# One staggered stage for spectrum, frequency gate and gated inverse, in place of three stages with a barrier after each

## The chip, the cores and the metric

The kernel runs on one core of a Trainium2 chip. The metric is the device time of one execution in microseconds (us), smaller is better. TensorE is called PE here as in the profile (its weight loads PEld), VectorE DVE, ScalarE ACT, GpSimd POOL; SP issues the DMAs.

## The reference

Four layers follow each other on x of shape (4, 64, 128, 128), float32. The change touches only the head of the first:

```
spec    = rfft2(x, norm='ortho')                    # 128 x 65 frequencies for each of 256 channel images
hid     = gelu(einsum('bchw,oc->bohw', abs(spec), fg_w1))      # 64 -> 16 channels at each frequency
gate    = sigmoid(einsum('bchw,oc->bohw', hid, fg_w2))         # 16 -> 64 channels
x_gated = irfft2(spec * gate, s=(h, w), norm='ortho')
xf      = x + x_gated
```

Everything after it (two patch convolutions of xf, an attention, the other three layers) is the same code before and after.

## The kernel before

The program is a sequence of stages. Each is a `Stage` with its own buffers and semaphores; at its end POOL clears the semaphores and all engines meet at a barrier, so no stage overlaps the next. Within a stage each engine runs its own instruction stream in order, and semaphores are the only link between them. `turns(eng, n)` emits the body once and then as a hardware loop for the other n - 1 turns.

The images lie in units of four (`G4`), 64 units in all, two units (s = 0, 1) a turn, 32 turns. A transform is two products with constant matrices of cosines and sines. `spectrum` loads a unit of x, multiplies it on the row axis by `c_h` (256 columns: 128 cosines and 128 sines), copies the result by ACT (L153), multiplies on the column axis by `c_w` (L141 and L142, 130 columns: 65 real and 65 imaginary), copies it by DVE (L169), squares it by ACT (L158), adds the squares by DVE (L173) and stores spectrum and power in DRAM. `frequency_gate` loads the power of all images with the channels of two images on the partitions, takes the root (L235), and runs the two channel products 416 frequencies at a time (L219, L228), Gelu and Sigmoid between them. `gated_inverse` loads spectrum, gate and x, multiplies (L315, two products of 128x260 a unit), transforms back over the rows with 256 output columns (L334, L335), ACT copies (L354), transforms over the columns with 65 rows of coefficients in two products (L342, L343), and DVE adds x (L322) while it reads PSUM.

All products are float32, and each appears in the trace as two matrix instructions, called passes below. One of 128x128 takes two passes, and so on.

## Time and profile before

| | |
|---|---|
| time, median of three runs | 8322.75 us (8309.79 to 8329.18) |
| the profiled execution: its time, its span | 8315.14 us, 8313.0 us |
| mean granted PE clock | 0.913 |
| `spectrum` | 0 to 280 us |
| `frequency_gate` | 280 to 422.5 us |
| `gated_inverse` | 422.5 to 870.5 us |
| all that follows | 870.5 to 8313 us |

The boundaries of the stages are the first DMA issue of the next one. The span is that of the trace. PEclk is the clock that the throttle granted to PE as a share of 2.4 GHz: 1.00 is 2.4 GHz and 0.50 is 1.2 GHz.

### The profile page before, as it was taken

Reading aid. Unit: us, or ns where it says so; the run is one execution under the profiler, and the core shown is the slowest. Engines: PE = TensorE matmul, PEld = TensorE weight load, DVE = VectorE, ACT = ScalarE, POOL = GpSimd, SP = SyncE. Lnnn points to the kernel's source line nnn. Section 1 sums busy time; section 2 is a strip of 40 time slices with the busy share of each in tenths; the row PEclk is TensorE's granted clock in tenths of the full one; section 3 lists DMA queues with packets and bytes.
Section 4 is the critical chain, followed back from the end, with each engine's and each line's share of the span. In section 5 each row is a group of like instructions: output and inputs, shape, how many; then the busy total and the mean of one; then the engine's idle time right before and its main releaser. Section 6 shows DMA issues by size and latency. Waiting matters only on the chain. (4 is left out here: it accounts for less than half of the span.)

```text
span 8313.0 us, 125384 instructions
## 1 busy us (share of the span) xinstructions
PE 7145.2 (86%) x38346; PEld 3824.7 (46%) x38346; DVE 5721.2 (69%) x5544; ACT 4038.9 (49%) x6602; POOL 3554.7 (43%) x2395
## 2 busy tenths in 40 slices
PE   8688584999999645987799999999989999999980
PEld 7356261333332542457422222222247777777760
DVE  2011014777776134831399999999979999999975
ACT  3411014666666124730266666666645555555532
POOL 0000000222222030000277777777768888888860
PEclk9788797999999877995699999999989999999995
DMA  9455526333333573343200000000000000000016
GB/s 154 125 140 137 106 50 221 94 102 98 100 100 92 128 241 111 102 133 91 47 14 14 14 14 13 14 14 14 9 14 11 10 9 9 9 10 9 10 28 190
DMA packets 724163, 582.48 MB, mean 70 GB/s; under 512 B 293562, under 2 KB 631105, under 8 KB 716505
## 3 DMA queue, kind: packets, MB, share of 16 engines
q1 hardware_dynamic: 723993, 580.38, 26.8%
q8 instruction: 87, 1.43, 0.1%
q14 instruction: 83, 0.68, 0.0%
HBM read 379.73 MB, written 197.83 MB: 69 GB/s over the span
## 5 line engine op out<-in xcount | busy, mean ns | idle before, releaser
L2646 POOL TENSOR_TENSOR spe_hc<-spe_hs,spe_cu 128x1024 f32<-128x1024 f32 x552 | 1289.6, 2358 | 293.8 <-DVE spe_hs L2843 293.8
L2242 POOL TENSOR_TENSOR spa_hc<-spa_hs,spa_cr 128x966 f32<-128x966 f32 x592 | 1224.7, 2069 | 426.7 <-DVE spa_hs L2516 410.6
L2516 DVE TENSOR_TENSOR_SCAN spa_hs<-spa_p_d,spa_hs,spa_bx 128x483 f32<-128x483 f32 x1168 | 1362.4, 1210 | 0.0
L2843 DVE TENSOR_TENSOR_SCAN spe_hs<-spe_p_d,spe_bx 128x1024 f32<-128x1024 f32 x552 | 1232.3, 2274 | 8.6 <-ACT spe_p_d L2792 7.9
L2720 PE MATMUL spe_p_y<-spe_idt,spe_hc 128*128 128x128 f32 x8832 | 1034.8, 276 | 0.0
L2720 PEld LDWEIGHTS spe_p_y<-spe_idt,spe_hc 128*128 128x128 f32 x8832 | 1012.0, 193 | 0.0
L1037 DVE TENSOR_REDUCE attention_nm<-attention_p_s 128x2 f32<-128x640 f32 x1024 | 789.0, 812 | 258.6 <-PE attention_p_s L894 257.5
L995 ACT ACTIVATE attention_pr<-attention_p_t 128x512 f32<-128x512 f32 x1280 | 710.6, 598 | 413.8 <-PE attention_p_t L917 285.7
L2427 ACT ACTIVATE spa_p_d<-spa_p_d,spa_av 128x483 f32<-128x483 f32 x1184 | 705.1, 634 | 409.5 <-PE spa_p_d L2299 407.5
L2792 ACT ACTIVATE spe_p_d<-spe_p_d 128x896 f32<-128x896 f32 x552 | 472.8, 900 | 845.8 <-PE spe_p_d L2705 845.4
L2299 PE MATMUL spa_p_d<-spa_du,spa_hot 32*128 32x483 f32 x2368 | 644.5, 619 | 58.0 <-DVE spa_hs L2516 48.8
L2502 DVE TENSOR_TENSOR spa_bx<-spa_br,spa_p_u 128x952 f32<-128x952 f32 x592 | 666.5, 1126 | 33.6 <-PE spa_p_u L2312 33.6
L2832 DVE TENSOR_TENSOR spe_bx<-spe_cu,spe_p_bc 128x2048 f32<-128x2048 f32 x276 | 631.5, 2288 | 51.8 <-ACT spe_cu L2784 17.0
L2312 PE MATMUL spa_p_u<-spa_du,spa_hot 32*128 32x483 f32 x2368 | 647.1, 621 | 0.7 <-DVE spa_bx L2502 0.5
L894 PE MATMUL attention_p_s<-attention_ks,attention_qs 96*128 96x320 bf16 x2048 | 454.5, 303 | 37.0 <-DMA attention_qs<-scratch_qp 20.9
L2299 PEld LDWEIGHTS spa_p_d<-spa_du,spa_hot 32*128 32x128 f32 x2368 | 182.1, 184 | 523.0 <-DVE spa_hs L2516 360.6
L1100 POOL TENSOR_TENSOR attention_on<-attention_os,attention_rc 128x512 f32<-128x512 f32 x128 | 162.6, 1270 | 589.4 <-DMA attention_rc<-scratch_den 379.4
L934 PE MATMUL attention_p_o<-attention_pr,attention_vs 128*32 128x512 f32 x3072 | 410.0, 606 | 0.4 <-ACT attention_os L1009 0.4
L917 PE MATMUL attention_p_t<-attention_qs,attention_ks 99*128 99x512 bf16 x1024 | 395.7, 387 | 4.7 <-DMA attention_qs<-attention_mr 3.0
L2705 PE MATMUL spe_p_d<-spe_wa,spe_dt 32*128 32x512 f32 x2208 | 376.0, 640 | 2.8 <-DVE spe_hs L2843 2.8
L415 POOL MEMSET conv_wb<- 128x4096 f32 x1 | 3.5, 3512 | 870.1 <-POOLq L38 870.1
L1869 PE MATMUL experts_p_x<-experts_fs,experts_wx 128*128 128x512 f32 x768 | 332.8, 596 | 47.4 <-DVE experts_bx L1895 47.4
(413 smaller groups left out, 11256.9 us busy)
## 6 DMA issues: line engine op xcount, KB each, us to landing
attention_qs<-scratch_qp SPq DMA_DIRECT2D x768, 64.0 KB, 2.6
attention_rc<-scratch_den SPq DMA_DIRECT2D x128, 256.0 KB
scratch_qp<-queries_parts SPq DMA_DIRECT2D x96, 256.0 KB, 2.3
spa_xt<-scratch_x SPq DMA_DIRECT2D x148, 121.5 KB, 2.6
scratch_spec<-spectrum_spc SPq DMA_DIRECT2D x64, 260.0 KB, 4.6
inverse_spec<-scratch_spec SPq DMA_DIRECT2D x64, 260.0 KB, 3.7
spectrum_xs<-in_x_dram SPq DMA_DIRECT2D x64, 256.0 KB, 5.1
inverse_xs<-in_x_dram SPq DMA_DIRECT2D x64, 256.0 KB, 3.3
```

Of the source, the lines that this page charges most:

```text
L995: nc.scalar.activation(pr[:, v, :], p_t[v % 2][:, :], ACT.Exp, scale=HD ** -0.5).then_inc(exp_done[v % 2], 1)
L1037: nc.vector.tensor_reduce(nm[:, c.u, t, 2 * s:2 * s + 2], p_s[s][:, :, 0:NK], AX.X, ALU.max, negate=True).then_inc(s_max[s], 1)
L2242: nc.gpsimd.tensor_tensor(hc[:, k % 8:k % 8 + 2, :], hs[:, k:k + 2, :], cr2[:, s % 2, :].unsqueeze(1).broadcast_to([128, 2, NA]), ALU.mult ...
L2299: mm = nc.tensor.matmul(p_d[(2 * j + e) % 4][:, 0:NA], hot[v, j // 2, :], du[v, s % 2, 0, :], start=True, stop=True)
L2312: mm = nc.tensor.matmul(p_u[:, e, 0:NA], hot[v, j // 2, :], du[v, s % 2, 1, :], start=True, stop=True)
L2427: nc.scalar.activation(p_d[k % 4][:, 0:NA], p_d[k % 4][:, 0:NA], ACT.Exp, scale=av2[:, k:k + 1]).then_inc(decay_ready, 1)
L2502: nc.vector.tensor_tensor(kept(bx[:, 2 * j:2 * j + 2, :]), b, kept(p_u[:, :, 0:NA]), ALU.mult).then_inc(bx_ready, 1)
L2516: nc.vector.tensor_tensor_scan(hs[:, k, v], p_d[k % 4][:, v], bx[:, k, v], 0.0 if start else hs[:, k, NA - 1:NA], ALU.mult, ALU.add).then_ ...
L2646: nc.gpsimd.tensor_tensor(hc[:, k, :, d, :].rearrange("p s d t -> p d s t"), hs[:, k % 2, d, :, :], rows, ALU.mult)\
L2720: mm = nc.tensor.matmul(p_y[:, px], hc[:, k, n].rearrange("p d t -> p (d t)"), idt[:, :], start=False, stop=(n == ST - 1))
L2832: nc.vector.tensor_tensor(bx[:, k % 2], steps, rows, ALU.mult).then_inc(bx_ready, 1)
L2843: nc.vector.tensor_tensor_scan(hs[:, k % 2, d].rearrange("p d s t -> p (d s t)"), p_d[h][:, :], bx[:, k % 2, d].rearrange("p d s t -> p (d ...
```

## The change

The three stages become one, `gated_frequencies`, a fully unrolled sequence of 97 steps with one unit u = t of the forward part and one unit v = t - 31 of the inverse part in step t. The gate of image b (16 units, u = 16b to 16b + 15) is spread over the half-steps k = 2t and 2t + 1 by `slot`: the root, nine turnings of the magnitudes by a product with the identity (`turn`, which brings the channels of two frequencies at a time onto the partitions), nine first channel products with Gelu, nine second products with Sigmoid.

- Spectrum, power and gate stay in SBUF: `spec` is a ring of 32 units, `mg` holds the power, magnitude and gate of three images, frequency-major, so that `by_image` reads and writes it with a stride of 64 elements (256 bytes).
- Of the row frequencies only 0 to 64 (cosines) and 1 to 63 (sines) are computed, 128 columns in place of 256. ACT unfolds them by symmetry with four copies in place of one.
- In the inverse the gated spectrum is laid out as 128 real and imaginary coefficients for each row frequency, so that the first product has 128 output columns and the second takes 128 rows of coefficients in one product. DVE makes that layout with four products in place of two.
- POOL adds 1 to the gate, and x is no longer loaded and added: the inverse of spec * (1 + gate) is x + x_gated.
- `p_spec`, `p_cols` and `p_img` have one buffer each where there were two.

The removed functions are printed above; the lines below are those added.

```
@@ -66,292 +66,325 @@
+KH = H // 2
+FP = 8
+NFG = -(-WF // FP)
+NU = B * C // G4
+UB = C // G4
+RING = 32
+LAG = 31
+def gated_frequencies(nc, x, c_h, c_w, ident, w1, w2, c_k, c_f, xf):
...
+    STEPS = NU + LAG + 2
+    with Stage(nc, "front") as st:
...
+        xs = st.sb("xs", [128, 4, G4, W])
+        spec = st.sb("spec", [128, RING, G4, 2 * WF])
+        mg = st.sb("mg", [128, 3, WF * C])
...
+        gs = st.sb("gs", [128, 2, 2, G4, 128])
...
+        p_rows = [st.ps(f"p_rows{s}", [128, G4, 128]) for s in range(2)]
+        p_spec = st.ps("p_spec", [128, 2, 512])
+        p_cols = st.ps("p_cols", [128, G4, 128])
+        p_img = st.ps("p_img", [128, G4, W])
+        p_g = [st.ps(f"p_g{s}", [128, 512]) for s in range(2)]
...
+        def by_image(b):
+            return mg[:, b % 3, :].rearrange("p (f n) -> p n f", n=C)
...
+        def slot(k):
+            b, i = divmod(k, 2 * UB)
+            return b - 1, i - 4
...
+            for t in range(STEPS + 1):
+                u, v = t + 3, t - LAG - 2
+                if u < NU:
+                    if u >= 4:
+                        sp.wait_ge(rows_done, u - 3)
+                    load(u)
+                if of(v, NU):
+                    sp.wait_ge(img_copied, v + 1)
+                    sp.dma_start(ov[:, G4 * v:G4 * v + G4, :], out[:, v % 2]).then_inc(stored[v % 2], 16)
...
+            for n in range(B * NFG):
+                b, g = divmod(n, NFG)
+                w = min(FP, WF - FP * g) * C
+                pool.wait_ge(gate_rough, n + 1)
+                v = mg[:, b % 3, FP * C * g:FP * C * g + w]
+                nc.gpsimd.tensor_scalar(v, v, 1.0, None, ALU.add).then_inc(gate_ready, 1)
+            pe.wait_ge(consts_in, 16 * 7)
+            def rows_of(u):
+                pe.wait_ge(x_in[u % 4], 16 * (u // 4) + 16)
+                if u >= 2:
+                    pe.wait_ge(rows_copied, 4 * (u - 1))
+                for i in range(G4):
+                    mm = nc.tensor.matmul(p_rows[u % 2][:, i, :], xs[:, u % 4, i, :], ch[:, :], start=True, stop=True)
+                mm.then_inc(rows_done, 1)
+            def spectrum_of(u):
+                pe.wait_ge(rows_copied, 4 * (u + 1))
+                if u >= 1:
+                    pe.wait_ge(spec_copied, u)
...
+                    nc.tensor.matmul(o, rows[:, u % 2, i, 0:128], cw[:, 0, :], start=True, stop=False)
+                    mm = nc.tensor.matmul(o, rows[:, u % 2, i, 128:256], cw[:, 1, :], start=False, stop=True)
+                mm.then_inc(spec_done, 1)
+            def columns_of(v):
+                pe.wait_ge(gated, 4 * (v + 1))
+                if v >= 1:
+                    pe.wait_ge(cols_copied, v)
...
+                    nc.tensor.matmul(p_cols[:, i, :], gs[:, v % 2, 0, i, :], ck[:, 0, :], start=True, stop=False)
+                    mm = nc.tensor.matmul(p_cols[:, i, :], gs[:, v % 2, 1, i, :], ck[:, 1, :], start=False, stop=True)
+                mm.then_inc(cols_done, 1)
+            def image_of(v):
+                pe.wait_ge(cols_copied, v + 1)
+                if v >= 1:
+                    pe.wait_ge(img_copied, v)
...
+                    mm = nc.tensor.matmul(p_img[:, i, :], cols[:, v % 2, i, :], cf[:, :], start=True, stop=True)
...
+            def turn(b, g):
+                n = b * NFG + g
+                if g == 0:
+                    pe.wait_ge(rooted, b + 1)
+                    if b >= 1:
+                        pe.wait_ge(gate_rough, n)
+                if n >= 1:
+                    pe.wait_ge(mt_copied, n)
+                for q, m in pairs(g):
+                    f = (FP * g + 2 * q) * C
+                    mm = nc.tensor.matmul(p_g[0][0:m * C, 128 * q:128 * q + 128], mg[:, b % 3, f:f + m * C], idt[:, :], start=True, stop=True)
+                mm.then_inc(turned, 1)
...
+                n = b * NFG + g
+                pe.wait_ge(mt_copied, n + 1)
+                if n >= 1:
+                    pe.wait_ge(hid_ready, n)
...
+                    mm = nc.tensor.matmul(p_g[1][32 * q:32 * q + 32, 0:128], w1s[0:m * C, :], mt[0:m * C, n % 2, 128 * q:128 * q + 128],
...
+                n = b * NFG + g
+                pe.wait_ge(hid_ready, NFG * (b + 1))
+                if n >= 2:
+                    pe.wait_ge(gate_rough, n - 1)
...
+                nc.tensor.matmul(p_g[g % 2][:, 0:w], hid[0:r, g, :], w2s[0:r, 0:w], start=True, stop=True).then_inc(gate_done, 1)
+            def gates(k):
+                b, i = slot(k)
+                if of(b, B):
+                    if of(i - 1, NFG):
+                        hidden(b, i - 1)
+                    if of(i, NFG):
+                        turn(b, i)
+                    if of(i - NFG - 2, NFG):
+                        gate(b, i - NFG - 2)
+            for t in range(STEPS):
+                u, v = t, t - LAG
+                if u < NU:
+                    rows_of(u)
+                if of(v, NU):
+                    columns_of(v)
+                gates(2 * t)
+                if of(u - 1, NU):
+                    spectrum_of(u - 1)
+                if of(v - 1, NU):
+                    image_of(v - 1)
+                gates(2 * t + 1)
...
+                nc.scalar.activation(r[:, :, 0:KH + 1], p[:, :, 0:KH + 1], ACT.Copy).then_inc(rows_copied, 1)
+                nc.scalar.activation(r[:, :, KH + 1:H], p[:, :, 1:KH], ACT.Copy).then_inc(rows_copied, 1)
+                nc.scalar.activation(r[:, :, H + 1:H + KH], p[:, :, KH + 1:H], ACT.Copy).then_inc(rows_copied, 1)
+                nc.scalar.activation(r[:, :, H + KH + 1:2 * H], p[:, :, KH + 1:H], ACT.Copy, scale=-1.0).then_inc(rows_copied, 1)
...
+                act.wait_ge(spec_copied, u + 1)
...
+                nc.scalar.activation(sq[:, u % 2], spec[:, u % RING], ACT.Square).then_inc(squared, 1)
+            def root(b):
+                act.wait_ge(summed, UB * (b + 1))
+                nc.scalar.activation(mg[:, b % 3, :], mg[:, b % 3, :], ACT.Sqrt).then_inc(rooted, 1)
...
+                nc.scalar.activation(cols[:, v % 2], p_cols[:, :, :], ACT.Copy).then_inc(cols_copied, 1)
...
+                nc.scalar.activation(hid[0:p, g, :], p_g[1][0:p, 0:128], ACT.Gelu).then_inc(hid_ready, 1)
...
+                nc.scalar.activation(mg[:, b % 3, FP * C * g:FP * C * g + w], p_g[g % 2][:, 0:w], ACT.Sigmoid).then_inc(gate_rough, 1)
+            def gates(k):
+                b, i = slot(k)
+                if of(b, B):
+                    if i == -1:
+                        root(b)
+                    if of(i - 2, NFG):
+                        gelu(b, i - 2)
+                    if of(i - NFG - 3, NFG):
+                        sigmoid(b, i - NFG - 3)
+            act.wait_ge(zeroed, 1)
+            for t in range(STEPS):
+                u, v = t, t - LAG
+                if of(u - 2, NU):
+                    square(u - 2)
+                if u < NU:
+                    copy_rows(u)
+                if of(v, NU):
+                    copy_columns(v)
+                gates(2 * t)
+                gates(2 * t + 1)
...
+                nc.vector.tensor_copy(spec[:, u % RING].rearrange("p (a i) f -> p a i f", a=2), pv).then_inc(spec_copied, 1)
...
+                dve.wait_ge(squared, u + 1)
...
+                nc.vector.scalar_tensor_tensor(by_image(b)[:, G4 * j:G4 * j + G4, :], sq[:, u % 2, :, 0:WF], 1e-34, sq[:, u % 2, :, WF:2 * WF],
+                                               ALU.max, ALU.add).then_inc(summed, 1)
+            def apply_gate(v):
+                b, j = divmod(v, UB)
+                dve.wait_ge(gate_ready, NFG * (b + 1))
+                if v >= 2:
+                    dve.wait_ge(cols_done, v - 1)
+                g, s = by_image(b)[:, G4 * j:G4 * j + G4, :], spec[:, v % RING]
+                re, im = s[:, :, 0:WF], s[:, :, WF:2 * WF]
+                a, c = gs[:, v % 2, 0], gs[:, v % 2, 1]
+                nc.vector.tensor_tensor(a[:, :, 0:WF], re, g, ALU.mult).then_inc(gated, 1)
+                nc.vector.tensor_tensor(a[:, :, WF:128], im[:, :, 1:WF - 1], g[:, :, 1:WF - 1], ALU.mult).then_inc(gated, 1)
+                nc.vector.scalar_tensor_tensor(c[:, :, 0:WF], im, -1.0, g, ALU.mult, ALU.mult).then_inc(gated, 1)
+                nc.vector.tensor_tensor(c[:, :, WF:128], re[:, :, 1:WF - 1], g[:, :, 1:WF - 1], ALU.mult).then_inc(gated, 1)
...
+                    nc.vector.tensor_copy(mt[:, n % 2, :], p_g[0][:, :]).then_inc(mt_copied, 1)
...
+                dve.wait_ge(img_done, v + 1)
...
+                nc.vector.tensor_copy(out[:, v % 2], p_img[:, :, :]).then_inc(img_copied, 1)
...
+            for t in range(STEPS):
+                u, v = t, t - LAG
+                if of(v + 1, NU):
+                    apply_gate(v + 1)
+                gates(2 * t)
+                if of(u - 1, NU):
+                    copy_spectrum(u - 1)
+                if of(u - 2, NU):
+                    add_squares(u - 2)
+                if of(v - 1, NU):
+                    copy_image(v - 1)
...
+    k["fg1"], k["fg2"] = twice(p("fg_w1").T), twice(twice(twice(p("fg_w2").T)))
+    k["c_h"] = np.concatenate([co[:, :65], si[:, 1:64]], 1)
+    kk = np.concatenate([np.arange(65), -np.arange(1, 64)]) % 128
+    k["c_k"] = np.stack([co[kk], si[kk]], 1)
+    k["c_f"] = np.concatenate([al * co[:WF], (-al * si[:WF])[1:WF - 1]], 0)
+    gated_frequencies(nc, *of("x c_h c_w ident fg1 fg2 c_k c_f xf"))
```

## Rows read from the trace of the kernel before

**Rows 1.** The page: span, and busy time of each engine.

```profile
span 8313.0 us, 125384 instructions
PE 7145.2 (86%) x38346; PEld 3824.7 (46%) x38346; DVE 5721.2 (69%) x5544; ACT 4038.9 (49%) x6602; POOL 3554.7 (43%) x2395
```

**Rows 2.** Windows of the three stages: busy us (x instructions), PE clock, DMA share, GB/s.

```profile
0.00:280.00 280.00, 235.66 (x1536) 215.89 (x1536) 69.31 (x128) 107.61 (x130) 0.20 (x4) 0.99 0.92 152
280.00:422.50 142.50, 88.37 (x160) 29.24 (x160) 0.00 (x0) 59.01 (x85) 0.00 (x0) 0.62 0.28 120
422.50:870.50 448.00, 391.39 (x2048) 280.24 (x2048) 87.70 (x192) 65.29 (x64) 0.00 (x0) 0.87 0.52 133
```

**Rows 3.** Waits, 0 to 870 us: us in total, times, longest.

```profile
PE inverse_p_cols L334 <- DVE inverse_gs L315: 73.2, 32, 28.0
DVE spectrum_spc L169 <- DMA scratch_power<-spectrum_pw: 53.3, 30, 4.8
```

**Rows 4.** Timeline in the spectrum stage: start us, us, what, [idle before].

```profile
155.32 3.72 PE L133 MATMUL spectrum_p_rows<-spectrum_ch,spectrum_xs 128*128 128x256 f32 x16 [0.66 <-DMA spectrum_xs<-in_x_dram]
```

**Rows 5.** Timeline in the inverse stage, round the start of a turn.

```profile
639.74 1.02 ACT L354 ACTIVATE inverse_cols<-inverse_p_cols 65x1024 f32<-65x1024 f32 x1 [9.18 <-PE inverse_p_cols L335]
...
647.37 1.44 DVE L315 TENSOR_TENSOR inverse_gs<-inverse_spec,inverse_gate 128x260 f32<-128x260 f32 x4
648.19 1.12 PE L334 MATMUL inverse_p_cols<-inverse_ck,inverse_gs 128*65 128x256 f32 x2 [1.46 <-DVE inverse_gs L315]
...
652.33 0.59 PE L334 MATMUL inverse_p_cols<-inverse_ck,inverse_gs 128*65 128x256 f32 x2
...
653.39 1.02 ACT L354 ACTIVATE inverse_cols<-inverse_p_cols 65x1024 f32<-65x1024 f32 x1 [9.18 <-PE inverse_p_cols L335]
```

**Rows 6.** Timeline late in the kernel: float32 passes of 128x128 by 128 columns.

```profile
8061.37 2.84 PE L2720 MATMUL spe_p_y<-spe_idt,spe_hc 128*128 128x128 f32 x24
```

**Rows 7.** Groups by line, 0 to 870 us: busy us, mean ns.

```profile
L153 ACT ACTIVATE spectrum_rows<-spectrum_p_rows 128x1024 f32<-128x1024 f32 x64 | 65.6, 1024 | 56.7 <-PE spectrum_p_rows L133 56.7
L169 DVE COPY spectrum_spc<-spectrum_p_spec 128x520 f32<-128x520 f32 x64 | 44.8, 700 | 191.6 <-PE spectrum_p_spec L142 138.3 <-DMA scratch_power<-spectrum_pw 53.3
L158 ACT ACTIVATE spectrum_sq<-spectrum_spc 128x520 f32<-128x520 f32 x64 | 40.8, 637 | 107.1 <-DVE spectrum_spc L169 107.1
L173 DVE SCALAR_TENSOR_TENSOR spectrum_pw<-spectrum_sq 128x260 f32<-128x260 f32 x64 | 27.2, 425 | 11.7 <-ACT spectrum_sq L158 11.7
L245 ACT ACTIVATE gate_mg<-gate_p_gate 128x416 f32 x38 | 19.6, 517 | 32.4 <-PE gate_p_gate L228 32.4
L235 ACT ACTIVATE gate_mg<-gate_mg 128x8320 f32<-128x8320 f32 x2 | 14.3, 7136 | 14.9 <-DMA gate_mg<-scratch_power 14.9
L240 ACT ACT_TABLE_LOAD x1 | 1.3, 1283 | 0.0
```

**Rows 8.** ACT groups, 2850 to 2880 us: strided (L1336) and contiguous (L1330) output.

```profile
L1336 ACT ACTIVATE mlp_os<-mlp_p_o,mlp_bs 128x512 f32<-128x512 f32 x8 | 8.2, 1117 | 1.3 <-PE mlp_p_o L1319 1.3
L1330 ACT ACTIVATE mlp_hid<-mlp_p_h,mlp_bs 128x512 f32<-128x512 f32 x8 | 5.5, 687 | 15.8 <-PE mlp_p_h L1312 15.8
```

**Rows 9.** DVE groups, 3755 to 3765 us: strided (L2003) and contiguous (L1994) output.

```profile
L2003 DVE SCALAR_TENSOR_TENSOR modes_uv<-modes_neg,modes_hf,modes_re 128x1600 f32<-128x1600 f32 x1 | 3.0, 3049 | 0.0
L1994 DVE TENSOR_TENSOR modes_re<-modes_re,modes_im 128x1600 f32<-128x1600 f32 x1 | 1.8, 1825 | 0.0
```

**Rows 10.** DMA, 0 to 870 us: packets and bytes; issues with size and us to landing.

```profile
DMA packets 237826, 119.19 MB, mean 137 GB/s; under 512 B 72989, under 2 KB 237182, under 8 KB 237310
spectrum_xs<-in_x_dram SPq DMA_DIRECT2D x64, 256.0 KB, 5.1
gate_w1s<-in_fg_dram SPq DMA_DIRECT2D x1, 16.0 KB, 1.7
```

**Rows 11.** DMA of instructions in the attention stage, 1300 to 2700 us: blocks, MB, share.

```profile
q8 instruction: 32, 0.52, 0.2%
```

**Rows 12.** The page: a GpSimd product of 128x512.

```profile
L1100 POOL TENSOR_TENSOR attention_on<-attention_os,attention_rc 128x512 f32<-128x512 f32 x128 | 162.6, 1270 | 589.4 <-DMA attention_rc<-scratch_den 379.4
```

More of the change, by code:

```diff
@@ new lines, in gated_frequencies @@
+        (turned, mt_copied, hid_done, hid_ready, gate_done, gate_rough, gate_ready) = (
+            st.sem(n) for n in ("turned", "mt_copied", "hid_done", "hid_ready", "gate_done", "gate_rough", "gate_ready"))
+        (gated, cols_done, cols_copied, img_done, img_copied) = (
+            st.sem(n) for n in ("gated", "cols_done", "cols_copied", "img_done", "img_copied"))
+        pv = p_spec[:, :, 0:4 * WF].rearrange("p a (i f) -> p a i f", i=2)
+        def by_image(b):
+            return mg[:, b % 3, :].rearrange("p (f n) -> p n f", n=C)
@@ L107, in _ @@
[L107 to L121 removed]
+            for dst, src in ((ch[:, :], c_h), (cw[:, :, :], c_w), (idt[:, :], ident), (w1s[:, :], w1), (w2s[:, :], w2), (ck[:, :, :], c_k),
+                             (cf[:, :], c_f)):
+                sp.dma_start(dst, src).then_inc(consts_in, 16)
@@ new lines, in pairs @@
+            def pairs(g):
+                return [(q, min(2, WF - FP * g - 2 * q)) for q in range(4) if FP * g + 2 * q < WF]
+            def turn(b, g):
[10 more added lines that the diff above has]
+                mm.then_inc(turned, 1)
@@ L145, in _, with copy_rows @@
         @block.scalar
         def _(act):
-            @turns(act, N)
-            def _(j):
-                for s in range(2):
-                    act.wait_ge(rows_done[s], j + 1)
-                    act.wait_ge(spec_done[s], j)
-                    nc.scalar.activation(rows[:, s], p_rows[s][:, :, :], ACT.Copy).then_inc(rows_copied[s], 1)
-                for s in range(2):
-                    act.wait_ge(spec_copied[s], j + 1)
-                    act.wait_ge(summed[s], j)
-                    nc.scalar.activation(sq[:, s], spc[:, s], ACT.Square).then_inc(squared[s], 1)
+            def copy_rows(u):
+                act.wait_ge(rows_done, u + 1)
+                if u >= 2:
+                    act.wait_ge(spec_done, u - 1)
+                r, p = rows[:, u % 2], p_rows[u % 2]
+                nc.scalar.activation(r[:, :, 0:KH + 1], p[:, :, 0:KH + 1], ACT.Copy).then_inc(rows_copied, 1)
+                nc.scalar.activation(r[:, :, KH + 1:H], p[:, :, 1:KH], ACT.Copy).then_inc(rows_copied, 1)
+                nc.scalar.activation(r[:, :, H + 1:H + KH], p[:, :, KH + 1:H], ACT.Copy).then_inc(rows_copied, 1)
+                nc.scalar.activation(r[:, :, H + KH + 1:2 * H], p[:, :, KH + 1:H], ACT.Copy, scale=-1.0).then_inc(rows_copied, 1)
@@ L3267, in of @@
         return [t[n] for n in names.split()]
-    spectrum(nc, *of("x c_h c_w spec power"))
-    frequency_gate(nc, *of("power fg1 fg2 gate"))
-    gated_inverse(nc, *of("x spec gate c_k c_f xf"))
+    gated_frequencies(nc, *of("x c_h c_w ident fg1 fg2 c_k c_f xf"))
     patch_convolutions(nc, *of("xf sr1 sr2 srb xs"))
```

300 lines of the change are left out of this document (74 added, 226 removed).

## The prediction

> **What bounds the kernel now.** The page comes first: PE is busy 86% of an 8313.0 us span [rows 1], but only the head is touched, so the windows of its three stages decide, and they hold 870.5 us [rows 2]. Three different limits stand there. In `spectrum` (280 us) the DMA engines are busy 0.92 of the time at 152 GB/s; the waits show DVE held 53.3 us by the store of the power [rows 3], and each turn's first products wait for x, 0.66 us in the turn shown [rows 4]. In `frequency_gate` (142.5 us) two bulk loads come before any work and two bulk stores after it, PE is busy 88.37 us, and its clock is at 0.62 [rows 2]. In `gated_inverse` (448 us) DMA is at 0.52 and PE busy 391.39 us at clock 0.87: a turn lasts 653.39 - 639.74 = 13.65 us, and PE waits 1.46 us in it for L315 [rows 5], 73.2 us in 32 turns, 28.0 of them before the first [rows 3]. Behind that wait two passes take 1.12 us, where two later ones in the turn take 0.59 us [rows 5]: PE falls to 1.2 GHz after the wait and returns to 2.4. In the spectrum stage a wait of 0.66 us leaves 16 passes of 256 columns at 3.72 us [rows 4], 0.22 us apart, and the window's clock at 0.99: so short a wait costs only itself.
>
> **Unit prices.** 24 passes by 128 columns take 2.84 us [rows 6]; with an end of some 0.27 us that is 0.1115 us a pass. A pass of 256 columns is 0.22 us apart, so one of 512 is put at 0.43. ACT from PSUM: 1024 elements 1024 ns, 416 elements 517 ns [rows 7], so 0.17 us + 0.83 ns an element. DVE: 520 elements from PSUM 0.70 us [rows 7]; four products of 260 elements 1.44 us, 0.36 each [rows 5].
>
> **PE of the new stage.** A unit takes 8 passes for its rows, 16 for its spectrum, 16 for the columns and 8 for the image: 0.89, 1.78, 1.78, 0.89, together 5.35 us. Before, a unit took (16 x 0.22 + 32 x 0.1115) / 2 = 3.55 us in the spectrum stage and (32 x 0.22 + 32 x 0.1115) / 2 = 5.3 us in the inverse, 8.85 us: the halved columns and the 128-row product save 3.5 us a unit, 224 us at full clock. An image's gate takes 33 turning and 33 hidden products (132 passes, 14.7 us) and 9 gate products (17 passes near 0.43, 7.3 us): 22 us.
>
> **DVE and the stride.** `add_squares` writes, and `apply_gate` reads, with 256 bytes between elements. The trace has such an output on ACT, 1117 ns against 687 ns for the same shape [rows 8], and one on DVE with 16 bytes between elements, 3049 ns against 1825 for as many elements [rows 9]: 0.84 and 0.77 ns an element more, close to twice the rate-bound part. Neither shows a strided input. Bounds: 0.36 us a product if it is free, 0.63 if each of 260 elements takes 1.04 ns more; I take 0.63, as the output rows are the nearest. So four products take 2.5 us a unit, the squares' sum 0.425 + 0.20 to 0.27 = 0.65.
> The trace's rows speak for the doubling by themselves. The Trainium skill (SBUF — State Buffer, "Door 1: The DMA port swizzle") says that every access that crosses to a new 16-byte line pays a penalty, and gives no size; by it both the sum and the products pay, which the rows agree with for outputs.
> DVE then needs 0.70 (spectrum) + 0.65 + 2.5 + 0.69 (image, 512 elements) = 4.55 us a full step, and 9 x 0.69 = 6 us an image for turned magnitudes. Below PE's 5.35 in a full step; above PE's 2.67 in a step with the inverse alone, 3.2 and with semaphore gaps 3.3.
>
> **ACT.** Four copies of 260 or 252 elements: 4 x 0.385 = 1.5 us for 1.02 before; square 0.64; columns (512) 0.60: 2.75 us a step. A gate adds the root (7136 / 2 = 3.6 us), 9 Gelu (0.28), 9 Sigmoid (0.60) and three table loads of 1.28 [rows 7]: 15.4 us an image. It lies beside PE except at two places. (a) `hidden(i - 1)` in half-step 2t waits for a Gelu that ACT issues behind `copy_rows` and `copy_columns` of the same step. In a forward-only step the rows end at 0.89 us, the four copies near 2.4, the Gelu at 2.7: PE waits 1.8 us. With both parts the columns end at 2.67, their copy and the Gelu 1.1 us later; at the end of the stage it is 1.0. That happens in four steps an image, and `spectrum_of`, `image_of` and the next rows queue behind it on PE. (b) The first `turn` waits for the root. From the end of the last spectrum come its copy 0.76, the sum 0.65, table load and root 4.9: 6.4 us, of which PE fills 0.9 with forward work alone and 3.5 with both parts: 5.7 and 3 us of wait; for the last image, where `apply_gate` stands ahead of the sum, I take 5. Each wait of 1 to 2 us costs some 1.7 us more at 1.2 GHz if it goes as at the start of the turn in [rows 5]; I put 1.6, 0.8 and 0.8 on each of (a), as the shorter ones may escape it, and 1.7 on each (b). So image 0 pays 4 x 3.4 + 7.4 = 21 us, images 1 and 2 each 4 x 1.9 + 4.7 = 12.5, image 3 4 x 1.8 + 6.7 = 14.
>
> **POOL and SP.** 36 additions on 512 elements, at most 1.27 us each [rows 12], come at one a half-step of 2.7 us or more, and the gate is wanted a step later: nothing; without that cover 11 us an image at most. SP issues one load of x three units ahead and one store a step; the store's wait for `img_copied` stands in front of the next load, but is met a step before. Of DMA, 119 MB [rows 10] become 34: 256 KB each way a step of 5 us or more is 100 GB/s, and 98 GB/s in a forward-only step, under the 152 reached before. What is removed is worth the stage it bounded, and is in the sum by that alone.
>
> **The sum.** Start: seven constants and x, 5 us before, put at 9. Steps 0 to 15: 16 x 2.68 = 43. Steps 16 to 30: 15 x 2.68 + 22 + 21 = 83. Steps 31 to 63: 33 x 5.35 + 2 x (22 + 12.5) = 246. Steps 64 to 75: spectrum 1.8, ten steps 27, gate 22 + 14: 65. The last 22 inverse steps, DVE's, 3.3 each: 73. Last store, clearing and barrier 5. In all 524 us for 870.5: 346 less. Against the profiled execution's own 8315.14 us that is 7969; the median of the runs is 7.6 us above it, so I say 7975. All that follows the stage finds the same xf and stays. The clock: PE has no wait over 0.7 us in the steps without a gate, so I expect 2.4 GHz there.
>
> **Rivals.**
> 1. *Strides free, waits covered.* 486 us: DVE gives back 22 x 0.6 = 13 us, and some 25 us of the waits under (a) and (b) are met by PE's queue. 7938. For it: the sum of PE's passes alone, with start and end, is 9 + 16 x 2.68 + 15 x 2.68 + 33 x 5.35 + 4 x 22 + 87 + 5 = 449, so the waits are my estimate and not a row. Against: the Gelu stands in program order behind the copies.
> 2. *Tables reloaded each step.* `Square` runs in every step, between Gelus or Sigmoids. Before, Copy and Square shared one load for 32 turns; no row shows Square with the table of Gelu, Sigmoid or Sqrt. If it is in none, each of some 10 steps in 3 images takes two more loads: 77 us of ACT, of which 1.3 us in 9 of 10 steps lands on (a) or the Sigmoids: 35 us, 8010.
> The Trainium skill (ScalarE: Activation LUTs, "Table sets: the hidden batching unit") wants calls grouped by set and names relu, copy, identity and abs as in every set, not Square; at its 2.7 us a switch these 60 loads would be an estimated 160 us of ACT. No row decides it; the trace has 1.283 us a load.
> 3. *DVE becomes the bound*, if a strided element costs three times, not twice: products 0.90, a step 0.70 + 0.9 + 3.6 + 0.69 = 5.9; 13 gate-free steps grow by 0.6 to 1, the last 22 by 1.1: 36 us, 8010.
> 4. *Instructions arrive late.* The stage is unrolled: 64 x 96 + 4 x 300 = 7300 PE instructions. In the attention stage 32 blocks came in 1400 us [rows 11] without an idle group of their own. At one small DMA's 1.7 us [rows 10] for each of 32 blocks: 54 us, 8030.
> 5. *Slower than before: the engines work in turn.* With one buffer for `p_spec`, `p_cols` and `p_img`, each product could wait for its own copy. The whole work laid end to end is 15.2 us in each of 33 full steps, 5.9 in 31, 6.5 in 33, and 86 for the first and last gate's operations: 985 + 14, 129 us slower, 8450. It decides from 870 / 97 = 9.0 us a mean step, that is once 73% of the overlap is lost. Against: PE always has a product of another part between a product and its next use of the buffer, 0.89 us behind `spectrum_of` in the shortest case, where the copy takes 0.70 and two semaphores.
>
> **How the numbers follow.** Forecast 0.58 (own range 7945 to 8005), rival 1 0.15, rival 2 0.09, rival 3 0.08, rival 4 0.06, rival 5 and the like 0.03; the remaining 0.01 is no change. A measurement of this kernel can tell about 0.2%, 17 us. The range takes in the centres of the forecast and of rivals 1 to 4, from 13 us below rival 1 to 15 above rival 4: 7925 to 8045. Each case scatters by some 30 us through the waits that I estimated, so that 2 in 10 still lie outside.
>
> **What would show it.** No `scratch_spec`, `scratch_power` or `scratch_gate` in the DMA list, the conv stage's first issue near 524 us in place of 870; a PE period of 5.3 us in gate-free steps with both parts, and of 3.3 at the end with DVE busy; `apply_gate` products near 0.7 us each; three table loads an image (12 in all); PE waits for ACT at `hidden` and at the first `turn`. Wrong if PE waits in gate-free steps, if table loads number some 70, or if a later stage moves.

## The result and the profile after

The changed kernel takes 7993.44 us, the median of 4 runs (7990.72 to 7999.3), against 8316.44 (8309.79 to 8329.18, 4 runs) before: a ratio of 0.9613, with a 95% interval of 0.9599 to 0.9627. The forecast was 7975 us with a range of 7925 to 8045. The profiled execution took 7999.3 us, of which 7997.2 is the span. The page's first lines, which answer to [rows 1]:

```profile
span 7997.2 us, 123173 instructions
PE 6916.9 (86%) x38274; PEld 3725.9 (47%) x38274; DVE 5842.8 (73%) x5708; ACT 4018.5 (50%) x6797; POOL 3606.3 (45%) x2432
```

PE's share is still 86%: a kernel can lose 316 us of span and keep the share of its main engine. From here on "the head" is everything ahead of the conv stage's first DMA issue: three stages before, one after. The windows of the head by phase (columns as in [rows 2]) show what took the place of the three stages:

```profile
0.00:9.00 9.00, 0.25 (x1) 0.28 (x2) 0.00 (x0) 0.00 (x0) 0.33 (x5) 1.00 0.62 175
9.00:60.00 51.00, 50.07 (x383) 47.62 (x384) 17.88 (x29) 28.79 (x82) 0.00 (x0) 1.00 0.31 88
60.00:140.00 80.00, 67.60 (x537) 59.56 (x536) 29.84 (x47) 41.87 (x101) 12.14 (x9) 0.96 0.18 53
...
330.00:390.00 60.00, 54.91 (x460) 51.27 (x459) 38.17 (x70) 26.77 (x52) 6.70 (x6) 0.97 0.18 54
390.00:494.00 104.00, 93.47 (x758) 84.24 (x757) 79.03 (x138) 23.04 (x44) 13.04 (x9) 0.99 0.24 74
```

The next stage issues its first DMA at 494.45 us, where it was at 870.5. The DMA share is 0.18 to 0.31 behind the start, so that bound is gone. PE's mean clock is 0.96 to 1.00 where the inverse was at 0.87 and the gate at 0.62; the granted clock reads 1.00 but for three stretches, which come up below. PE's waits in the head answer to [rows 3]:

```profile
PE front_p_g L229 <- ACT front_hid L300: 23.3, 16, 3.0
PE front_p_g L220 <- ACT front_mg L285: 9.4, 4, 4.1
PE front_p_rows L175 <- DMA front_xs<-in_x_dram: 8.7, 1, 8.7
PE front_p_g L239 <- ACT front_mg L306: 1.6, 2, 0.9
```

Of 494 us PE waits 45 for a named releaser, 43 of them in these four rows. Groups by line of the same stretch, which answer to [rows 7] and [rows 12]:

```profile
L164 POOL TENSOR_SCALAR front_mg<-front_mg 128x512 f32<-128x512 f32 (+1 forms) x36 | 49.5, 1389 | 384.1 <-ACT front_mg L306 384.1
...
L339 DVE SCALAR_TENSOR_TENSOR front_mg<-front_sq 128x260 f32<-128x260 f32 x64 | 40.9, 638 | 0.0
...
L350 DVE TENSOR_TENSOR front_gs<-front_spec,front_mg 128x260 f32<-128x260 f32 x64 | 39.2, 612 | 0.0
...
L229 PE MATMUL front_p_g<-front_mt,front_w1s 128*32 128x128 f32 (+1 forms) x264 | 15.5, 287 | 23.3 <-ACT front_hid L300 23.3
...
L285 ACT ACT_TABLE_LOAD x4 | 5.1, 1283 | 0.1
L300 ACT ACT_TABLE_LOAD x4 | 5.1, 1283 | 0.1
L306 ACT ACT_TABLE_LOAD x4 | 5.1, 1283 | 0.1
```

The DMA of the head, which answers to [rows 10]: 34.88 MB for 119.19.

```profile
DMA packets 68634, 34.88 MB, mean 71 GB/s; under 512 B 2288, under 2 KB 68465, under 8 KB 68593
...
front_xs<-in_x_dram SPq DMA_DIRECT2D x64, 256.0 KB, 2.9
```

The head gives back 376.0 us, but the span only 315.8. The stages behind it tell where the other 60.2 went. Each is cut at one DMA issue of the next stage, the same one before and after (in some stages smaller loads go out up to 17 us ahead of it). In us, before and after:

| stage | before | after | difference |
|---|---|---|---|
| head | 870.5 | 494.5 | -376.0 |
| conv, queries, attention | 1837.7 | 1838.0 | +0.3 |
| first low-rank stage (`low`) | 120.5 | 126.1 | +5.6 |
| mlp, inv, resid, feats | 403.9 | 406.1 | +2.2 |
| experts and second `low` | 512.6 | 524.5 | +11.9 |
| modes, spatial Mamba | 2369.7 | 2369.0 | -0.7 |
| spectral Mamba (`spe`) | 1973.0 | 2013.7 | +40.7 |
| merge | 225.1 | 225.3 | +0.2 |

One stage, which the change does not touch, has two thirds of it. Its window and its instruction DMA, before:

```profile
6114.90:8087.90 1973.00, 1930.65 (x13250) 1468.92 (x13250) 1888.55 (x908) 1060.32 (x1729) 1628.62 (x828) 0.99 0.04 10
```
```profile
q8 instruction: 27, 0.44, 0.1%
```

and after:

```profile
5758.20:7771.90 2013.70, 1954.18 (x13250) 1475.01 (x13250) 1890.20 (x908) 1062.92 (x1729) 1631.09 (x828) 0.98 0.05 11
```
```profile
q8 instruction: 144, 2.36, 0.5%
```

The work is the same, 13250 passes on PE and 908 instructions on DVE; queue 8, the instruction queue of [rows 11], brings 144 blocks in place of 27. Waits of the stage, before:

```profile
PEld spe_p_d L2705 <- issue: 10.6, 9, 2.6
...
DVE spe_hs L2843 <- ACT spe_p_d L2792: 7.9, 2, 4.7
```

and after:

```profile
DVE spe_hs L2876 <- ACT spe_p_d L2825: 45.9, 16, 4.6
PEld spe_p_d L2738 <- issue: 35.3, 22, 2.5
...
PE spe_p_d L2738 <- issue: 14.0, 13, 1.3
```

PE's weight loads for `spe_p_d` wait 35.3 us for "issue", time for which the profile shows no releaser, where it was 10.6, and DVE's scans wait 45.9 us, where it was 7.9, for the ACT copy behind those very products. The last row has no counterpart before: 13 pauses, and the stage is a hardware loop with 14 turns. A late instruction has no name in this view.

### The profile page after: what moved, and what is told of

Its sections match the earlier page's. It is cut to its first block and busy times, and to the rows that moved or that the text cites. A ratio compares the mean times of both kernels' runs of the same rounds, so it can differ in the third digit from the quotient of the medians.

```text
span 7997.2 us, 123173 instructions
## 1 busy us (share of the span) xinstructions
PE 6916.9 (86%) x38274; PEld 3725.9 (47%) x38274; DVE 5842.8 (73%) x5708; ACT 4018.5 (50%) x6797; POOL 3606.3 (45%) x2432
## 5 line engine op out<-in xcount | busy, mean ns | idle before, releaser
L2549 DVE TENSOR_TENSOR_SCAN spa_hs<-spa_p_d,spa_hs,spa_bx 128x483 f32<-128x483 f32 x1168 | 1634.5, 1676 | 0.0
L2876 DVE TENSOR_TENSOR_SCAN spe_hs<-spe_p_d,spe_bx 128x1024 f32<-128x1024 f32 x552 | 1232.8, 2275 | 46.6 <-ACT spe_p_d L2825 45.9
L2535 DVE TENSOR_TENSOR spa_bx<-spa_br,spa_p_u 128x952 f32<-128x952 f32 x592 | 938.2, 1585 | 33.7 <-PE spa_p_u L2345 33.7
L2359 PE MATMUL spa_p_y<-spa_hc,spa_fd 128*32 128x483 f32 x2368 | 303.6, 585 | 5.4 <-POOL spa_hc L2275 4.2
```

The source lines that it names most:

```text
L2535: nc.vector.tensor_tensor(kept(bx[:, 2 * j:2 * j + 2, :]), b, kept(p_u[:, :, 0:NA]), ALU.mult).then_inc(bx_ready, 1)
L2549: nc.vector.tensor_tensor_scan(hs[:, k, v], p_d[k % 4][:, v], bx[:, k, v], 0.0 if start else hs[:, k, NA - 1:NA], ALU.mult, ALU.add).then_ ...
L2876: nc.vector.tensor_tensor_scan(hs[:, k % 2, d].rearrange("p d s t -> p (d s t)"), p_d[h][:, :], bx[:, k % 2, d].rearrange("p d s t -> p (d ...
```

## The experiments

**Why does an untouched stage take 41 us more?** Counted in the compiled programs (not in a trace): PE's loop in that stage is 1647 instructions, run 14 times, and the new head has 7107 PE instructions more, which moves where the loop begins. A block of the instruction queue is 2.36 / 144 = 0.0164 MB. The Trainium skill (Runtime: NRT & Kernel Launch, "Instruction fetch mechanics") gives a block as 16 KiB or 256 instructions, and the trace's size agrees. In such blocks the loop is 6.43 long. Theory P (placement): depending on where it begins it touches 7 blocks or 8, and with 8 PE refetches some on each repeat; 144 - 27 = 117 is 9 for each of 13 repeats, as many as the pauses above. The rival: something that the new stage itself does or leaves behind. The loop began at 0.891 of a block before and begins at 0.652 now.

**e1: the changed kernel, 96 PE instructions more in a place where PE is idle.** Before the conv stage's first product PE waits 90.5 us for `conv_x`; ahead of that wait it now waits over and over for a semaphore that is already met (two waits go into one instruction).

```diff
-            pe.wait_ge(zeroed, 2)
+            for _ in range(193):
+                pe.wait_ge(zeroed, 2)
```

> The changed kernel with 96 more instructions in PE's stream, repeated waits on a semaphore that is already met, placed in the convolution stage where PE waits 90.5 us for its input. Theory P (placement): spectral_mamba's loop of 1647 PE instructions refetches its instruction blocks in every turn, since its place in the stream moved; 96 instructions more put it back inside one block less. Expect 27 blocks on the q8 instruction queue in that stage in place of 144, the stage 1973 us long in place of 2014, the whole 41 us shorter, about 7952 us. Rival Q (what the new stage leaves behind, in clock, memory or buffers, slows the later stages): no change, 7993 us, 144 blocks. Under both, the new stage itself stays at 494 us.

Measured: 7947.85 us (7940.19 to 7958.38), 0.9564 of before (0.9548 to 0.958). The spectral stage takes 1972.8 us and the head 494.8.

```profile
5709.10:7681.90 1972.80, 1925.83 (x13183) 1456.47 (x13180) 1894.58 (x911) 1060.74 (x1732) 1634.16 (x831) 0.98 0.04 10
```
```profile
q8 instruction: 26, 0.43, 0.1%
```

96 idle instructions make the kernel 46 us faster, and the stage that lost 40.7 us has 40.9 of them back. (The profiled span is 59 us shorter; most of the other 18 lie in the `low` stages and in modes, 306.7 for 313.9.) P stands, and for this stage its rival falls: the new stage is in this kernel as before.

**e2: the same with 8 instructions,** the control: it moves the loop by 0.03 of a block, to 0.684.

```diff
-            pe.wait_ge(zeroed, 2)
+            for _ in range(17):
+                pe.wait_ge(zeroed, 2)
```

> The same edit with 8 instructions in place of 96, as a control. Theory P: 8 instructions, 0.03 of a block, leave the loop where it straddles one block more: 144 blocks and 2014 us in spectral_mamba, 7993 us in all. Rival R (any disturbance of the stream resets the chance pattern): time between 7952 and 7993 us.

Measured: 8009.34 us (2 runs), ratio 0.9633 (0.9614 to 0.9653); 144 blocks, the stage 2045.6 us. So it is the place and not the padding. The price of a bad place is not a constant: 41 us in the changed kernel, 73 here.

**e3: the kernel before, 195 instructions more at the same point,** so that its loop begins at 0.652 too.

```diff
-            pe.wait_ge(zeroed, 2)
+            for _ in range(391):
+                pe.wait_ge(zeroed, 2)
```

> The kernel before with 195 more PE instructions at the same idle place of the convolution stage; nothing of the new stage is in it. They bring spectral_mamba's loop to the place within a block that it has in the changed kernel (0.652 of a block). Theory P: spectral_mamba grows from 1973 to 2014 us with 144 blocks in place of 27, the whole is 41 us slower than before, some 8357 us. Rival Q: no change, 8316 us.

Measured: 8351.33 us (8341.47 to 8353.99) for 8317.98, ratio 1.0042 (1.0027 to 1.0056). The head stays (871.7 us for 870.5), the spectral stage goes from 1973.0 to 2004.4, and its blocks from 27 to 144.

None of the change is in this kernel. Over the ten kernels of this study the stage has 26 or 27 blocks and 1973 us where the loop begins at 0.891, 0.027, 0.043 or 0.152 of a block (four kernels), and 143 or 144 blocks and 2004 to 2046 us at 0.645 to 0.684 (six). A loop of 6.43 blocks fits in 7 if it begins in the first 0.57 of one; the good values fit that if the true block edge lies some 0.11 to 0.32 before the counted one. That offset was not measured, and 7 blocks against 8 is the reading that fits, not one that a view shows. The same page of the Trainium skill says in that section that a taken branch to a target outside the sequencer's window of two pages has to fetch it before execution goes on. In the bad places the 13 repeats agree, but a window of two blocks does not fit: in the good places a loop of 6.43 blocks repeats 13 times, and the stage still has only 26 or 27 blocks. What fits better is the 128 KiB of instruction memory, 8 such blocks, that the Trainium skill gives PE in the same section. Of straight code the Trainium skill says in the same section that crossing a block is mostly hidden, which the head bears out: 30 blocks, and full steps without a gate take 5.36 us for a forecast of 5.35.

**e4: the arithmetic alone.** The kernel before with its three stages and its trips through HBM, but with half the row frequencies, the four copies and the 128-row inverse. Does the gain come from fewer passes or from the fusion?

```diff
-    ch = st.sb("ch", [128, 256])
+    ch = st.sb("ch", [128, 128])
...
-    gs = st.sb("gs", [128, 2, G4, 2 * WF])
-    cols = st.sb("cols", [WF, 2, G4, 256])
+    gs = st.sb("gs", [128, 2, 2, G4, 128])
+    cols = st.sb("cols", [128, 2, G4, 128])
...
-    nc.tensor.matmul(p_img[s][:, i, :], cols[:, s, i, 0:128], cf[:, 0, :], start=True, stop=False)
-    mm = nc.tensor.matmul(p_img[s][:, i, :], cols[:, s, i, 128:256], cf[:, 1, :], start=False, stop=True)
+    mm = nc.tensor.matmul(p_img[s][:, i, :], cols[:, s, i, :], cf[:, :], start=True, stop=True)
```

> The kernel before with the arithmetic of the change alone, in its three stages and with spectrum, power and gate still in DRAM: 128 columns for the rows with four unfolding copies, 128-row inverse with four gate products; x is still loaded and added. Theory D (DMA bounds the spectrum stage, the wait for the gate products and PE the inverse): spectrum stage stays within 3 us of 280, the gate stage 142, the inverse falls from 448 to about 32 x 8 + 8 = 265 us, so 180 us of the 376 that the head gained come from the arithmetic and 195 from the fusion. Rival (the arithmetic is most of it): spectrum 170, inverse 180, 350 us gained. By theory P its loop in spectral_mamba begins at 0.645 of a block and should refetch too, plus 41 us: 8316 - 180 + 41 = 8177 us.

Measured: 8193.82 us (8187.47 to 8197.3), ratio 0.9853 (0.9836 to 0.9869); head 713.7. The windows answer to [rows 2]:

```profile
0.00:282.00 282.00, 208.23 (x1536) 198.49 (x1536) 69.29 (x128) 117.35 (x322) 0.33 (x5) 0.91 0.91 151
...
424.00:714.00 290.00, 212.15 (x1536) 206.08 (x1536) 130.15 (x320) 38.21 (x64) 0.34 (x1) 0.88 0.77 205
```

Of 376 us the arithmetic alone gives 157 and the rest of the change, the fusion with what it removes, the other 219. In `spectrum` the smaller products change nothing, as DMA bounds it (0.91, 151 GB/s). The inverse falls from 448 to 290, 25 above what I expected. The timeline of a turn shows why:

```profile
561.29 0.49 PE L346 MATMUL inverse_p_cols<-inverse_ck,inverse_gs 128*128 128x128 f32 x2 [2.12 <-DVE inverse_gs L328]
...
562.98 0.63 PE L347 MATMUL inverse_p_cols<-inverse_ck,inverse_gs 128*128 128x128 f32 x2
...
566.15 0.39 PE L346 MATMUL inverse_p_cols<-inverse_ck,inverse_gs 128*128 128x128 f32 x2
...
570.73 0.49 PE L346 MATMUL inverse_p_cols<-inverse_ck,inverse_gs 128*128 128x128 f32 x2 [2.12 <-DVE inverse_gs L328]
```

This turn lasts 9.44 us; PE waits 2.12 for DVE, and for some 3.2 us two passes take 0.64 where they take 0.39 later: the half clock again (the windows from 562 to 565 us are at 0.50). The wait answers to the 1.46 of [rows 5]. Not every turn falls: 17 of the 31 between the first wait and the last are such, the first of 10.38 us and 16 of 9.43 or 9.44, and the other 14 take 7.80 or 7.81 behind the same wait of 2.12. One fall costs 1.63 us, and 17 of them are 28, about the 25 that the inverse takes beyond the expected.

**e5: the Gelu ahead of the copies.** Point (a) of the prediction, undone: ACT issues the first gate operations of a step before `copy_rows` and `copy_columns`.

```diff
+                gates(2 * t)
                 if u < NU:
                     copy_rows(u)
                 if of(v, NU):
                     copy_columns(v)
-                gates(2 * t)
                 gates(2 * t + 1)
```

> The changed kernel with ScalarE's first half-step of the gate (which holds the Gelus and Sigmoids of even half-steps) ahead of the copies of rows and columns, not behind them. Theory G: PE's 23.3 us of waits for Gelus come from that program order alone, so they vanish and the head falls from 494 to some 472 us; PE's stream is the same length, so spectral_mamba keeps its 144 blocks and its 2004 to 2046 us. Whole: some 22 us less, about 7972 us. Rival: the wait moves to the copies of the rows or to spectrum_of, head 490 us or more.

Measured: 7947.42 us (7945.14 to 7948.02), ratio 0.9589 (0.9573 to 0.9605). (e5 to e8 ran on a chip on which the kernel before takes 8289.97 us, so their times compare with the changed kernel's by the ratios, 0.9613 for that one.) The head takes 465.8 us, 28.7 less; PE's wait for Gelu falls from 23.3 us to 0.6, and nothing takes its place: PE's largest waits for other engines are now

```profile
PE front_p_g L220 <- ACT front_mg L285: 9.4, 4, 4.1
PE front_p_rows L175 <- DMA front_xs<-in_x_dram: 8.5, 1, 8.5
```

22.7 us of waits for Gelu are gone, and with them the 1.6 for Sigmoid; of the 28.7 some 4 to 5 stay that no wait names. They are not the clock: the head loses 5.1 us to the half clock here and in the changed kernel alike (the sum of one less the granted clock over windows of 1 us, without the stage's end). The spectral stage is in its bad place (144 blocks, 2016.6 us).

**e6: the best version.** e5, with the padding of e1 and the root in two pieces, so that the first turning products wait for 512 of its 4160 elements. Of the edit, what is new:

```diff
+                if g < 2:
+                    pe.wait_ge(rooted, 2 * b + 1 + g)
                 if g == 0:
-                    pe.wait_ge(rooted, b + 1)
...
-                nc.scalar.activation(mg[:, b % 3, :], mg[:, b % 3, :], ACT.Sqrt).then_inc(rooted, 1)
+                for v in (mg[:, b % 3, 0:FP * C], mg[:, b % 3, FP * C:]):
+                    nc.scalar.activation(v, v, ACT.Sqrt).then_inc(rooted, 1)
```

> The same order, with 96 more PE instructions in the convolution stage, and the root in two pieces of 512 and 3648 elements so that the first turn waits for the first piece alone. Theory G and P: head 472 less 2 to 3 us for each of four images, 462 us; 27 blocks, 1973 us in spectral_mamba; whole 7948 - 32 = 7916 us. Rival: the second turn waits for the rest of the root just as long, head 472 us.

Measured: 7892.72 us (7881.91 to 7903.25), ratio 0.9518 (0.9502 to 0.9534) for the changed kernel's 0.9613: by the ratios 79 us of 8316 better than the changed kernel. Waits for the root are 1.4 us in place of 9.4, and the spectral stage has 27 blocks and 1973.2 us. The head takes 454.0 us, 8 less than I expected. The clock explains it: no window of 1 us in this head is below full clock ahead of the stage's end. Against e5, 8.0 us of waits for the root and 5.1 of half clock less, and 1.1 more of Gelu waits, are 12.0 for a measured 11.8. e5 took away the waits for Gelu alone and kept its 5.1 us.

**e7: the gate read in a contiguous order.** `apply_gate` takes other elements of the gate, which lie side by side; the products have the same size.

```diff
-                g, s = by_image(b)[:, G4 * j:G4 * j + G4, :], spec[:, v % RING]
+                g = mg[:, b % 3, :].rearrange("p (n f) -> p n f", n=C)[:, G4 * j:G4 * j + G4, :]
+                s = spec[:, v % RING]
```

> The changed kernel in which apply_gate reads the gate contiguously, so that it takes other elements of it than the right ones (the computation is changed there); the writes keep their stride. Theory S (a strided element costs about double, and DVE bounds the inverse-only steps alone): each of the four products falls from 0.61 us to about 0.42, the last 20 or so steps from a 2.86 us period to PE's 2.68, the head from 494 to 490 us. Rival: the stride costs the whole stage through DVE, head 470 us or less.

Measured: 7973.36 us (2 runs), ratio 0.962 (0.96 to 0.9639), head 492.4. Groups of the head, the first untouched, the second of the edit:

```profile
L339 DVE SCALAR_TENSOR_TENSOR front_mg<-front_sq 128x260 f32<-128x260 f32 x64 | 40.9, 639 | 0.0
...
L351 DVE TENSOR_TENSOR front_gs<-front_spec,front_mg 128x260 f32<-128x260 f32 x64 | 27.2, 426 | 0.0
```

A product goes from 612 to 426 ns, some 46 us of DVE in all, and the head gains 2.1. Only the last steps have DVE at the bound, and they go from 2.9 to 2.80 us. There the single buffer `p_cols` takes over: the last product into it, its copy by ACT (0.60 us, done at 477.74 in this trace) and the next product (477.88) follow each other.

**e8: the four hidden products into the same 32 partitions.** In the trace eight hidden passes take 0.43 us, where I had priced 0.89. Theory C (columns): each pass uses 32 of PE's 128 output columns, another 32 for each of four, and these run side by side. Its rival: a pass with 32 output columns is simply cheaper, wherever it writes.

```diff
-                    mm = nc.tensor.matmul(p_g[1][32 * q:32 * q + 32, 0:128], w1s[0:m * C, :], mt[0:m * C, n % 2, 128 * q:128 * q + 128],
+                    mm = nc.tensor.matmul(p_g[1][0:32, 128 * q:128 * q + 128], w1s[0:m * C, :], mt[0:m * C, n % 2, 128 * q:128 * q + 128],
```

The Gelu and the gate products then work on 32 partitions and four times the columns.

> The changed kernel with the four hidden products of a group put out to the same 32 partitions, in four stretches of 128 columns, and not to four groups of 32 partitions; the Gelu then reads 32x512 elements, and the gate product of 512 columns becomes four of 128 columns over 32 rows. Theory C (products into separate groups of 32 output partitions run at the same time): eight hidden passes take 0.89 us in place of 0.43, 15 us more over 33 groups of eight, and Gelus of 0.60 us in place of 0.28 add 5 us in PE's waits: head 514 us. Rival (the 32-column weights make them fast): eight passes stay at 0.43 us, head 499 us. PE's stream is 384 instructions longer, which by theory P puts the loop of spectral_mamba at 0.15 of a block: 27 blocks, 1973 us there.

Measured: 7974.05 us (2 runs), ratio 0.962 (0.9601 to 0.964), head 534.9. Before the edit and behind it, first the changed kernel and then e8, eight passes in the timeline:

```profile
91.09 0.43 PE L229 MATMUL front_p_g<-front_mt,front_w1s 128*32 128x128 f32 x8
91.44 1.16 PE L220 MATMUL front_p_g<-front_idt,front_mg 128*128 128x128 f32 x8
```
```profile
93.07 1.06 PE L229 MATMUL front_p_g<-front_mt,front_w1s 128*32 128x128 f32 x8
```

The next product starts 0.35 us behind the first of the eight, against 0.99 in e8, and the group's busy time goes from 15.5 to 36.3 us, with the same columns read by every pass. C stands. The head grows by 40.4 us: 20.8 in these passes, 4.7 in waits for Gelu, 3.9 in the gate products, which now are four small ones each, 2.3 in the turning passes; 8.7 remain. Part of them is the clock: by the same sum over windows of 1 us this head loses 11.9 us to it and the changed kernel's 5.1, and only the 2.3 in the turning passes are counted yet. Some 4 us I cannot place. This kernel's spectral stage has 27 blocks and 1973.0 us: its smaller gate products moved the loop to 0.152 of a block, as P wants, and that hides the longer head in the total, whose ratio is the changed kernel's.

## Why the prediction was right, and where it was not

The profiled execution took 7999.3 us where the sum said 7969. The 30 us are two errors of opposite sign: the head came out 29.5 us shorter than its 524, the stages behind it 60.2 us longer. That the total fell so near is luck: the head's 494.5 lies nearer to rival 1's 486, and e1, the same kernel with the spectral stage in its good place, takes 7947.85 us, nearer to rival 1's 7938 than to 7975, though rival 1's mechanism is wrong. The head by the terms of the sum, cut where ACT is released or starts its copy:

| term | forecast | measured |
|---|---|---|
| start, to the end of ACT's first wait | 9 | 10.9 |
| steps 0 to 15 | 43 | 48.7 |
| steps 16 to 30, with the first gate | 83 | 78.9 |
| steps 31 to 63, with two gates | 246 | 229.3 |
| steps 64 to 75, with the last gate | 65 | 65.5 |
| the last inverse steps | 73 | 55.8 |
| end | 5 | 5.3 |

**The step that failed: "All that follows the stage finds the same xf and stays."** The data are the same, but the program is one stream of instructions for each engine, and 7107 more of them on PE move a later loop against its blocks: +40.7 us, shown by e1, e2 and e3. Rival 4 named late instructions and gave them 0.06, but put them in the new stage, where none shows as a wait of its own, and priced them by blocks that arrive once, while the cost is in a loop that fetches the same ones again. "Or if a later stage moves" stood among the signs of a wrong prediction; it was the one that occurred. The two `low` stages have another 5.6 us (the first) and 12.7 (the second, 118.2 before and 130.9 after), with PE's clock lower in both (0.87 for 0.90, 0.80 for 0.90) and the same work. For the first stage and for modes the ten profiles scatter without relation to an edit (119.8 to 128.6 us, 293.9 to 314.8). The second does not: the three kernels with the old head (before, e3, e4) take 118.2 to 122.4 us in it, at a clock of 0.87 to 0.90, and the seven with the new one 124.7 to 130.9, at 0.80 to 0.86. So some 2 to 13 us there do go with the new head (one profile of each kernel), by a way that no run here shows; the cause stays open.

**Mis-sized: the hidden passes.** I took them at the 0.1115 us of any pass. Eight take 0.43 us and not 0.89, since four run side by side (e8): some 15 us in 264 passes.

**Mis-sized: the clock behind a wait.** The places of the waits were right: 23.3 us for Gelu in 16 waits of up to 3.0 (forecast 20), and 9.4 for the root in 4 (forecast 16.7). But I added the half clock of [rows 5] to each, some 23 us in all. It fell behind three of these 20 waits: a root wait of 4.11 us, and two Gelu waits, of 2.98 and 2.37. The first two lines are one of them, the last two a wait behind which nothing falls (the hidden passes show it in neither case, the turning passes behind them do):

```profile
79.01 0.43 PE L229 MATMUL front_p_g<-front_mt,front_w1s 128*32 128x128 f32 x8 [2.98 <-ACT front_hid L300]
79.37 1.93 PE L220 MATMUL front_p_g<-front_idt,front_mg 128*128 128x128 f32 x8
...
87.85 0.42 PE L229 MATMUL front_p_g<-front_mt,front_w1s 128*32 128x128 f32 x8 [1.56 <-ACT front_hid L300]
88.21 1.16 PE L220 MATMUL front_p_g<-front_idt,front_mg 128*128 128x128 f32 x8
```
```profile
80.00:81.00 1.00, 1.00 (x7) 1.00 (x6) 0.00 (x0) 0.00 (x0) 0.00 (x0) 0.50 0.00 0
```

Each fall costs 1.7 us, as forecast, but three are 5.1 us and not 23. In the inverse before, waits of 1.46 us bring the half clock in every turn of 13.65 us; in e4 a wait of 2.12 us brings it in 17 turns of 31; here 1.56 us does not in any of three waits, and of three Gelu waits of 2.37 us one does. Neither their length nor their spacing parts the one case from the other, and no run here was made for it: what decides it stays open. Cheaper hidden passes and fewer falls of the clock together are what makes the two gates of steps 31 to 63 some 26 us each and not 34.5.

**Mis-sized: DVE's last steps,** 3.3 us each for a measured 2.9. A strided product takes 0.61 us, as taken from [rows 8] and [rows 9] (0.63), but the next one begins before it has ended, 0.51 behind it:

```profile
477.81 0.69 DVE L369 COPY front_out<-front_p_img 128x512 f32<-128x512 f32 x1 [0.20 <-PE front_p_img L202]
478.42 0.60 DVE L350 TENSOR_TENSOR front_gs<-front_spec,front_mg 128x260 f32<-128x260 f32 x1
478.94 0.59 DVE L351 TENSOR_TENSOR front_gs<-front_spec,front_mg 128x252 f32<-128x252 f32 x1
...
480.65 0.69 DVE L369 COPY front_out<-front_p_img 128x512 f32<-128x512 f32 x1
```

The durations of one group, added up, are more than the engine's time. The sum also counted 22 such steps, and only 20 lie behind the last gate: 20 x 0.5 and 2 x 3.3 are the 17 us.

**Mis-sized the other way: the forward steps,** 2.91 us and not 2.68. What the sum put at nothing is the single buffer `p_spec`. The case against rival 5 was that 0.89 us of rows lie between two spectra, where the copy takes 0.70 and two semaphores. The trace of one step:

```profile
22.94 0.39 PE L185 MATMUL front_p_spec<-front_cw,front_rows 128*128 128x130 f32 x2
23.17 1.05 PE L175 MATMUL front_p_rows<-front_ch,front_xs 128*128 128x128 f32 x8
24.21 0.46 PE L184 MATMUL front_p_spec<-front_cw,front_rows 128*128 128x130 f32 x2
```
```profile
23.37 0.70 DVE L334 COPY front_spec<-front_p_spec 128x520 f32<-128x520 f32 x1 [1.69 <-PE front_p_spec L185]
```

The spectrum ends at 23.33 us, its copy runs to 24.07, and the next spectrum starts at 24.21, though the rows between them would have let it start at 24.06 and ACT's four copies of its rows had ended at 22.91. With the slower first pair that is 0.23 us a step, 3 us over 13 steps. The other 3 of the 5.7 us lie in the first three steps: the spectrum waits 0.93 us for its first rows, and the first 40 passes are some 0.22 us apart and not 0.11, though the windows show the clock at 1.00 there. In steps with both parts the buffer costs nothing. This is read from the trace; no run gives `p_spec` a second buffer.

**Right.** A full step without a gate: rows begin at 252.97 and at 258.33 us, 5.36 us apart, forecast 5.35. The gate on PE, but for the hidden passes. The sum of squares with a strided output, 638 ns (0.65). The DMAs at 34.9 MB, all met. POOL's additions of 512 elements take 1.5 us and not 1.27, at no cost. Three table loads an image: none is caused by `Square`, which rival 2 had feared. Rival 1's free strides are refuted by e7 (612 for 426 ns), and its covered waits by e5; rival 3's triple price by the same product, and rival 5 by the 5.36, though its mechanism is what the forward steps pay for.

## What to carry to other kernels

Adding or removing unrolled instructions moves every later hardware loop of that engine: cut both traces into stages and compare the untouched ones too, with the count of instruction blocks beside each. Where a loop refetches, some idle instructions ahead of it, at a point where the engine waits anyway, can be worth more than a tuned operation: 41 to 46 us here. A single buffer needs more work between its two uses than the copy takes: 0.89 us of rows for a copy of 0.70 cost 0.23 us a step. When stages are fused, put what the next engine waits for ahead of what has slack in every engine's program; two lines exchanged gave 29 us.

## What the hardware showed

- PE's loop of 1647 instructions had 27 blocks or 144 over 14 iterations, by its place alone; the bad place cost 31 to 73 us.
- Four float32 products of 128 rows to 32 output columns, in four different column groups, run side by side: eight in 0.35 to 0.43 us, against 0.99 to 1.06 in one group.
- `Square` runs with the tables of Sqrt, Gelu and Sigmoid loaded: 13 table loads in the head, of 1.283 us each.
- A DVE product of 260 float32 with 256 bytes between the elements of one operand takes 612 ns for 426, an output so strided 638 for 425.
- Each fall to 1.2 GHz cost 1.6 to 1.7 us, but the same wait brought it in some turns and not in others: 2.12 us in 17 turns of 31 (e4), 2.37 us once in three times (the changed kernel).
- In the spatial Mamba, untouched too, DVE's scan at L2549 has a mean of 1676 ns where it was 1210 before, yet the stage takes 2054.9 and 2055.1 us. I have no cause for it, and no cost.
